# A decoder layer on one Trainium2 core: a shared-expert piece, a sum and a set of transposes moved in the last batches, and the last expert's down product in plain fp32

## What is computed

```python
x = x + self_attention(layernorm(x), Wq, Wkv, Wo, bo)          # windowed mask, ALiBi, 16 query heads, 4 kv heads
x = x + cross_attention(layernorm(x), ctx, ctx)                # 32 query heads of 16, 8 kv heads
h = layernorm(x)
choice, weight = gate(h)                                       # sigmoid scores; best 2 of 4 groups, best 4 experts there
out = moe(h, choice, weight, w1, w2, w3)                       # 32 experts, up to 128 tokens each
#   expert e: (silu(rows @ w1[e]) * (rows @ w3[e])) @ w2[e]    # 512 -> 256 -> 512
shared = (silu(h @ shared_gate) * (h @ shared_up)) @ shared_down   # 512 -> 512 -> 512
x = x + out + shared
```

## Time and profile before

| what | value |
|---|---|
| executions timed | 986.92, 985.15, 981.0 us; median 985.15 us |
| profiled execution | 981.55 us, of which the span is 979.4 us |
| mean granted TensorE clock | 0.971 of full speed |
| DMA | 114.70 MB in all |

### The profile page before, as it was taken

One profiled execution on the slowest core, in us unless ns is written; L12 is line 12 of the kernel. 1 busy time (PEld: TensorE's weight loads), 2 busy tenths in 40 slices (PEclk: granted clock), 3 DMA queues, 4 the chain that ended last, 5 costly groups with the idle time before them and its releaser, 6 DMA issues.

```text
span 979.4 us, 16786 instructions
## 1 busy us (share of the span) xinstructions
PE 906.3 (93%) x6300; PEld 572.2 (58%) x6300; DVE 650.4 (66%) x1464; ACT 385.1 (39%) x747; POOL 281.6 (29%) x286
## 2 busy tenths in 40 slices
PE   5897998999999999999999999988999899999994
PEld 5464546646745754764775575464477555655562
DVE  1477657857886785795787678585342277777773
ACT  4130363264265246326426524524500144444441
POOL 0302002110620530341062063033215244444332
PEclk9997698999999999999999999999999999999997
DMA  5465006003302300620340240083152499999832
GB/s 147 131 238 135 3 1 167 8 3 87 88 26 70 103 4 2 156 63 2 87 110 25 71 104 3 3 256 110 51 186 59 143 375 351 340 341 336 234 42 26
DMA packets 97315, 114.70 MB, mean 117 GB/s; under 512 B 11606, under 2 KB 72470, under 8 KB 97232
## 3 DMA queue, kind: packets, MB, share of 16 engines
q1 hardware_dynamic: 84340, 94.81, 31.1%
q0 software_dynamic: 9872, 16.07, 7.3%
q10 hardware_dynamic: 3024, 2.75, 1.1%
HBM read 70.90 MB, written 16.88 MB: 90 GB/s over the span
## 4 chain that ended last, share of the span: by engine, by line
PE 69%; DVE 16%; ACT 5%; issue 4%; SPq 3%; DMA 2%; POOL 0%; ACTq 0%; POOLq 0%; DVEq 0%
PE qa L1777 11%; PE qa L1620 6%; DVE mxx L1094 4%; PE qx L1555 4%; PE pt L1329 4%; PE vb L1566 4%; PE qa L1329 4%; PE qa L1411 4%; ACT arena L684 3%; PE qx L1497 3%; DVE mx L1062 2%; PE qa L1445 2%; PE va L1372 2%; PE qx L1762 2%; PE qx L1764 2%
## 5 line engine op out<-in xcount | busy, mean ns | idle before, releaser
L684 ACT ACTIVATE arena<-qx 128x512 f32<-128x512 f32 (+1 forms) x268 | 153.9, 603 | 136.1 <-PE qx L1555 115.0
L1094 DVE TENSOR_REDUCE mxx<-qx 128x2 f32<-128x512 f32 x256 | 168.0, 685 | 42.7 <-PE qx L1497 41.6
L684 ACT ACTIVATE arena<-qa 128x512 f32<-128x512 f32 (+2 forms) x124 | 66.2, 537 | 156.3 <-PE qa L1777 78.4
L1777 PE MATMUL qa<-arena 128*128 128x512 f32 x256 | 116.0, 596 | 0.9 <-ACT arena L684 0.9
L1497 PE MATMUL qx<-arena 96*128 96x256 bf16 x512 | 102.5, 290 | 15.2 <-DVE mxx L1094 10.6
L530 POOL TENSOR_TENSOR rstd<-mv,power 128x2 f32<-128x2 f32 x24 | 17.2, 715 | 334.9 <-DVE mv L930 334.9
L1555 PE MATMUL qx<-arena 98*128 98x512 bf16 x256 | 94.6, 391 | 6.9 <-ACT arena L684 2.9
L1566 PE MATMUL vb<-arena 128*32 128x256 f32 x1024 | 82.2, 393 | 1.6 <-ACT arena L684 0.4
L1497 PEld LDWEIGHTS qx<-arena 96*128 96x128 bf16 x512 | 46.5, 102 | 58.2 <-DVE mxx L1094 25.8
L1777 PEld LDWEIGHTS qa<-arena 128*128 128x128 f32 x256 | 46.2, 190 | 47.0 <-issue 47.0
L1329 PE MATMUL pt<-arena 128*128 128x256 f32 x256 | 70.8, 389 | 1.5 <-DVE res L1036 1.5
(11 more groups left out here) (251 smaller groups left out, 1728.4 us busy)
## 6 DMA issues: line engine op xcount, KB each, us to landing
arena<-in_L_ffn_w SPq DMA_DIRECT2D x96, 512.0 KB, 10.2
arena<-arena SPq DMA_DIRECT2D x75, 128.0 KB, 2.6
qs<-arena SPq DMA_DIRECT2D x24, 384.0 KB, 5.0
res<-in_x SPq DMA_DIRECT2D x8, 512.0 KB, 4.7
xnd<-arena SPq DMA_DIRECT2D x8, 512.0 KB, 5.9
ks<-arena SPq DMA_DIRECT2D x48, 64.0 KB, 1.9
arena<-arena SPq DMA_DIRECT2D x48, 64.0 KB
arena<-arena ACTq DMA_DIRECT2D x21, 128.0 KB, 3.5
```

The source lines that it names most:

```text
L684: nc.scalar.activation(dst, src, func, **kw).then_inc(s[signal], 1)
L1094: v_.reduce_max(mxx[:, col:col + 3:2], xbank[v % 2].rearrange("p (h n) -> p h n", h=2), AX.X).then_inc(s["x_max"], 1)
L1777: op = mm(abank[e % 2], xgt[e % 2][:, c, :], h13[e % EU][:, :, c, :], start=c == 0, stop=c == DC - 1)
```

## The change

There are four edits. (1) In body 8, piece 22 is done whole by eight steps ahead of the first score step, in `abank[0]`; pieces 23 to 25 follow one step behind each of the score steps 0 to 23, in `abank` in turn; no step is held over into the lead. TensorE's wait for `x2` ahead of piece 22 goes. ScalarE and GpSimd take piece 22 out ahead of their score loop. (2) In body 9, VectorE adds piece 34 between `choose_groups` and `choose_experts`. (3) The first expert's transposes (`bring(0)`) stand ahead of piece 47, which now goes to `abank[1]`, and the wait for all sums (`sh_added`) moves from ahead of `bring(0)` to expert 1. (4) For expert 31, ScalarE copies the transposed hidden once, in fp32; the split of weights and hidden falls away; the down product is two fp32 products of 512 columns, and it stands ahead of the last `shared_tokens`.

The transposes of expert 0 and piece 47 have changed places. The diff, cut to what the prediction speaks of:

```diff
@@ -245,3 +245,3 @@
         he = [view(arena, ht_at + DC * S + r * F, F) for r in range(2)]
-        hte = [view(arena, ht_at + r * 2 * P, 2 * P).rearrange("p (c n) -> p c n", c=2) for r in range(2)]
+        hte = view(arena, ht_at, 2 * P).rearrange("p (c n) -> p c n", c=2)
         ye = ([view(arena, ox_at + r * D, D) for r in range(4)] + [view(res, (2 * 4 + r) * D, D) for r in range(2)])
@@ -306,4 +306,8 @@
 
+            if i == PIECES - 1:
+                return abank[1]
             if i >= POOLED:
                 return abank[0] if i % 2 else pt[:, 512:1024]
+            if i >= FIRST_PIECE[B]:
+                return abank[i % 2]
             k = max(k for k in FIRST_PIECE if FIRST_PIECE[k] <= i)
@@ -322,4 +326,4 @@
 
-            at_ = v - (16 if k == 2 else 0)
-            if k in FIRST_PIECE and at_ >= 0 and at_ % PIECE_SLOTS == PIECE_SLOTS - 1:
+            at_ = v - (16 if k == 2 else 0) + (PIECE_SLOTS if k == B else 0)
+            if k in FIRST_PIECE and 0 <= at_ < XU and at_ % PIECE_SLOTS == PIECE_SLOTS - 1:
                 return [FIRST_PIECE[k] + at_ // PIECE_SLOTS]
@@ -608,2 +612,4 @@
                     add_bias(k)
+                if k == B:
+                    shared_out(FIRST_PIECE[B])
                 for v in range(XU):
@@ -770,2 +776,5 @@
 
+                if k == B:
+                    shared_copies(FIRST_PIECE[B])
+
                 def third_out(t):
@@ -900,2 +909,7 @@
                     act.wait_ge(s["down_done"], e)
+                hidden = va[:, 0:2 * P].rearrange("p (c n) -> p c n", c=2)
+                if e == NE - 1:
+                    act.wait_ge(s["ht_t"], e + 1)
+                    copy(hte, hidden, "ht_ready")
+                    continue
                 act.wait_ge(wg_in[e % EU], e // EU * 48 + 48)
@@ -903,3 +917,3 @@
                 act.wait_ge(s["ht_t"], e + 1)
-                copy(ht_hi, va[:, 0:2 * P].rearrange("p (c n) -> p c n", c=2), "ht_hi")
+                copy(ht_hi, hidden, "ht_hi")
             joined(NE // 2 - 1)
@@ -1135,5 +1149,6 @@
                     choose_groups()
-                    choose_experts()
                     if not x:
                         shared_out(POOLED + 8)
+                    choose_experts()
+                    if not x:
                         shared_out(POOLED + 9)
@@ -1231,2 +1246,4 @@
 
+                if e == NE - 1:
+                    return
                 if e > 0:
@@ -1475,3 +1492,3 @@
                         pe.wait_ge(s["c_rem"], k + 1)
-                    if n_ == 0:
+                    if n_ == 0 and a:
                         pe.wait_ge(s["x2"], k * 3 - 3)
@@ -1487,2 +1504,5 @@
                         pe.wait_ge(s["slot_ready"], k - 2)
+                    if not a:
+                        for n_ in range(PIECE_SLOTS):
+                            shared_slot(n_)
                     pe.wait_ge(s["kxs_in"], k * 96)
@@ -1519,3 +1539,3 @@
                             self_maxima()
-                        for n_ in STEPS.get(v, ()):
+                        for n_ in STEPS.get(v, ()) if a else range(v + PIECE_SLOTS, min(v + PIECE_SLOTS + 1, XU)):
                             shared_slot(n_)
@@ -1642,3 +1662,3 @@
                     for v in range(LEAD):
-                        for n_ in HELD[v] if v < len(HELD) else ():
+                        for n_ in HELD[v] if a and v < len(HELD) else ():
                             shared_slot(n_)
@@ -1756,3 +1776,4 @@
             def down(e):
-                pe.wait_ge(s["w2_split"], e + 1)
+                if e < NE - 1:
+                    pe.wait_ge(s["w2_split"], e + 1)
                 pe.wait_ge(s["ht_ready"], e + 1)
@@ -1760,2 +1781,7 @@
                     pe.wait_ge(s["y_ready"], e)
+                if e == NE - 1:
+                    for c in range(2):
+                        op = mm(xbank[0], hte[:, c, :], h2[e % EU][:, c, :], start=c == 0, stop=c == 1)
+                    op.then_inc(s["down_done"], 1)
+                    return
                 for c in range(2):
@@ -1766,7 +1792,9 @@
 
-            for i in range(POOLED + 10, PIECES):
+            for i in range(POOLED + 10, PIECES - 1):
                 shared_piece(i)
-            pe.wait_ge(s["sh_added"], B * 2)
             bring(0)
+            shared_piece(PIECES - 1)
             for e in range(NE):
+                if e == 1:
+                    pe.wait_ge(s["sh_added"], B * 2)
                 pe.wait_ge(wg_in[e % EU], e // EU * 48 + 48)
@@ -1792,4 +1820,4 @@
                     spread_ids(e // 2)
-            shared_tokens(NE // 2 - 1)
             down(NE - 1)
+            shared_tokens(NE // 2 - 1)
 
```

More of the change, by code:

```diff
@@ L1135, in _ @@
                     choose_groups()
+                    if not x:
+                        shared_out(POOLED + 8)
                     choose_experts()
                     if not x:
-                        shared_out(POOLED + 8)
                         shared_out(POOLED + 9)
@@ L1792, in _ @@
                     spread_ids(e // 2)
+            down(NE - 1)
             shared_tokens(NE // 2 - 1)
-            down(NE - 1)
 _INS = ["x", "ctx_512", "L0_attn_Wq", "L0_attn_Wkv", "L0_attn_Wo", "L0_attn_bo", "L0_ffn_gate_w", "L0_ffn_gate_bias",
```

## The result

The changed kernel takes 976.15 us (median of 16 executions, 973.51 to 980.85), the kernel before 981.42 us in the same count (979.97 to 986.92). The ratio is 0.9948, 95% interval 0.9929 to 0.9966: faster by half a per cent, less than one per cent. So sixteen executions tell half a per cent from no change, where the prediction put the limit at one. Forecast were 977 us, a range of 972 to 982.5, and within 1% with a chance of 0.78. The gain was put at 7.1 us; it is 5.3 by the medians.

The account below looks back on a forecast made before the run. TensorE was taken to bound the kernel: 93% busy, 69% of the last chain. 1.7 + 1.4 + 1.8 + 2.2 = 7.1 us off 981.55 (profiled) or 985.15 (median) gives 974.4 or 978.1; forecast 977, range 972 to 982.5.

Parts of the forecast that it names:

- Part 1: Body 8: with the held steps gone from the lead, piece 26 begins at about 672.5 instead of 674.30; 1.7 us won.
- rival 1: Clock falls between body 8's loops, up to 1.7 us lost, the first term pays nothing; 978.7 us, chance 0.17.
- the row at 669: Profile window of the kernel before, between body 8's loops: TensorE worked 0.11 us, clock still full; taken to say it stays full.
- the prediction's own sign: Body 8: the forecast is wrong if clock windows between 663 and 673 are below 1.00.
- about a third: Body 8's last eight score steps: TensorE works for about a third of VectorE's 0.63 us a step.
- The head: Start of body 8: piece 22's eight steps, 3.4 us, begin after the `slot_ready` wait at 640.42; nothing won by it.
- No edit moves that: Body 8: row copies stand behind twelve weight loads in SyncE's queue and land at 669.89, whatever the edits.
- rival 4: Body 8: row copies land later; slower once over 7.1 us later, 986 us at a landing time of 14.7; chance 0.04.
- Part 2: Body 9: piece 36 starts at 732.15 instead of 733.58, as the counts hardly wait; 1.4 us won, bounds 1.2 to 1.5.
- Part 3: Ahead of the experts: the first product follows piece 47 without a gap; 1.8 us won, 1.6 to 2.1.
- Part 4: Last expert: VectorE's last product starts at 964.75 instead of 966.96; 2.2 us won, 0.1 with the clock low throughout.
- Rival 3: Whole kernel: two more low-clock stretches of 1.7 us each go as well; gain 10.5, 974.6 us, chance 0.15.

Follow-up runs that it names:

- e4: Changed kernel plus two unread bf16 matmuls behind each of score steps 24 to 31 in body 8; 972.37 us against 981.63, ratio 0.9900.
- e9: Changed kernel with expert 3's three weight loads issued behind the row copies in SyncE's queue, no added matmuls; 980.02 us against 988.38, ratio 0.9918.
- e2: Kernel before with only body 8's new order of shared steps; 980.61 us against 981.63, ratio 0.9995.
- e10: Changed kernel run once more, unaltered, for a second profile; body 8 from its head to the scores behind piece 26 takes 40.40 us.
- e6: Changed kernel, but the last down product keeps its six split fp32r matmuls, ahead of the last sum of common rows; 976.98 us, one execution.
- e7: Changed kernel, but the plain fp32 last down product stands behind the last sum of common rows; 975.23 us, one execution.
- e8: Kernel before with only the sum of piece 34 moved between the two choices; 976.53 us, one execution.
- e11: Kernel before run once more, unaltered, for a second profile; body 8 from its head to the scores behind piece 26 takes 38.66 us.
- e12: Kernel before with only the row copies moved ahead of three weight loads in SyncE's queue; body 8's head to scores behind piece 26 takes 39.10 us.
- e3: Changed kernel with the 24 steps of pieces 23 to 25 behind score steps 8 to 31 instead of 0 to 23; 978.04 us, ratio 0.9924.
- e5: e4 with expert 3's three weight loads issued behind the row copies in SyncE's queue; 973.8 us against 981.64, ratio 0.9911.
- e1: Changed kernel with body 8 as it was before; 975.98 us against 981.63, ratio 0.9924.

## Why the prediction was right or wrong

**Part 1, predicted 1.7 us, got -1.2.** The step that failed is the choice between the two readings of the clock. The prediction saw the thin last eight steps, named their fall as rival 1, and followed "the row at 669 as the nearer one": there the clock was full after an idle stretch. But that idle stretch came behind a loop whose last steps still had shared matmuls between them; the row did not show the case that the change makes. By the prediction's own sign, clock windows below 1.00 between 663 and 673, this mechanism was wrong: the forecast of the total held, that of part 1 did not. And "about a third" was too low for the thin steps: TensorE is busy for 0.59 us in the window at 669, and loses its clock all the same. e4 and e9 settle it: work in the thin steps keeps the clock full through a wait of 1.71 us, and thin steps without any wait lose it. Rival 1's price, up to 1.7 us, was too small as well, since it took the 3.4 us of low clock at 642 for the length; it lasts about 10 us in three of the five profiles (changed, e2, e10) and about 7 in e6 and e7. R to S is 8.44 us in the changed kernel and 6.15 in e4: 2.3 us lost, against the 1.55 won (7.70 from the wait's end to S before, 6.15 in e4). In e7 it is 7.01: 0.9 us lost. The rule of the Trainium skill ("TensorE: Matmul & The Clock Gate", What's actually happening), that activity releases a throttled state which is the default, pointed to rival 1. e4 and e9 agree with it.

The head came as worked out: start behind `slot_u`, and no gain from it. "No edit moves that", of the row copies, may not quite hold: they land 31.6 to 31.9 us behind H with the new order and 30.7 to 31.6 with the old. That would be rival 4 in small, 0.7 us on average where it needed 7.1. Whether GpSimd's earlier write does it wasn't tried.

**Part 2, predicted 1.4, got 1.59** (24.69 - 23.10). The prediction allowed the count 0.3 us between the choice and piece 36; it takes 0.18.

**Part 3, predicted 1.8, got 2.1** (227.13 - 225.01), the upper end given: the product loses its own start, too.

**Part 4, predicted 2.2, got 2.08 in the profiled pair.** But 1.05 against e2 and e8, and 2.3 against e11 and e12. The base moves: 6.25 us was an execution in which the clock had fallen, as in e11 and e12; in e2 and e8 it hadn't, and the old ending takes 5.2. So the 2.2 us held for the profiled pair, and the prediction gave no size for a kernel before at full clock. The new ending takes 4.16 or 4.17 in all seven profiles that have it, at full clock. The path of the prediction (hidden 0.37, product 1.97, sum, copy, multiply) is what the rows show, one by one.

**Sum.** -1.2 + 1.6 + 2.1 + 1.0 to 2.3 is 3.5 to 4.8 us; the profiled pair has 341.10 - 336.07 = 5.0 from H on, the medians 5.3. What the medians have beyond the parts stays open. The medians mix executions that enter body 8 early and late (last section): by their times, seven of the changed kernel's sixteen are late ones (978.6 to 980.9) and four of the kernel before's (984.5 to 986.9). That the level came so close is luck: the gain was 1.8 us too large, and the base that 977 implies, 984.1, leaning on a median of three runs with two high ones (985.15), was 2.7 us above the 981.42 of sixteen. Rival 3 (more than told) did not come.

## What to carry to other kernels

When work is moved forward to fill a wait, look at what it leaves thin behind it. Here TensorE, left with small score matmuls for 0.6 of its time, lost its clock, and the price fell on the next dense stretch: 2.3 us (0.9 in the mildest profile) against 1.55 us won. Leftover work at the end of that loop (e3), or matmuls that nobody reads (e4), kept the clock. And copies of a few KB on which an engine waits are worth trying ahead of bulk loads in their queue: here they were worth 1.9 us with the loads of one expert behind them, where the loop ended ahead of them (e4 to e5).

## What the runs showed of the hardware

Two of the moves of the clock weren't expected. It fell during work, not idling (e9), and it stayed low for 10 us of which TensorE was busy for the last 6.

And the same code enters body 8 at two different times: at 636.4 to 638.6 in five profiles and at 642.3 to 642.9 in five others, those of e1 to e8 and of the first pair. It is decided within the first 51 us: one and the same matmul (`qa<-masks,identb`, L1583 before, L1603 in the changed kernel) starts at 45.78 in the kernel before and at 50.76 in the changed one. Windows of the kernel before (columns as above), once in its profiled execution and once in e11, which is the same program on another chip:

```profile
28.00:32.00 4.00, 4.00 (x6) 0.60 1.08 217
32.00:36.00 4.00, 3.23 (x20) 1.00 1.01 339
36.00:40.00 4.00, 3.49 (x26) 1.00 0.21 77
40.00:44.00 4.00, 3.41 (x10) 1.00 0.00 0
```

```profile
28.00:32.00 4.00, 3.99 (x10) 1.00 1.03 240
32.00:36.00 4.00, 1.49 (x11) 0.96 1.04 312
36.00:40.00 4.00, 4.00 (x17) 0.50 0.37 140
40.00:44.00 4.00, 3.25 (x15) 0.50 0.00 0
```

In the first the low clock lies at 28 to 32, in the second at 36 to 50. (e2 and e8 have a short stretch of it at 40 to 44 as well, and enter early.) The five late profiles all have the second form, the changed kernel's first profile among them; of the five early ones none has. On the chip of e9 to e12 everything up to body 8 takes longer, but the two forms are 4.8 to 6.6 us apart there too: e9 and e10 have the first and enter at 643.0 and 644.5, e11 and e12 have the second and enter at 649.6 and 649.3. The granted clock tells the forms apart in executions without a profile as well: in e3 it is 0.966 in the five at 978 us and 0.971 to 0.973 in the four at 972, in the sixteen of the changed kernel 0.963 to 0.965 in the seven at 978.6 to 980.9 and 0.968 to 0.971 in the nine at 973.5 to 976.4. Ten us more at 1.2 GHz would take 0.005 off the mean, an estimate, and that is the difference. So this is probably the larger part of the spread between executions. It wasn't tried what at the start decides it. A small gain should therefore be read from stretches that begin behind that point, or from many executions.
